# Where the attention masks are added: eight small matmuls per pair of heads' scores, or one VectorE addition on the way to SBUF

## The reference

```python
def local_attention(q, k, v):            # w = WINDOW = 32
    ...
    bk2, bv2 = (look(bk), look(bv))      # keys of the window before, then of this one: 64
    ...
    mask = (it < jb) | (it > jb + w) | (jb == -1)
    sim = jnp.einsum('bhwie,bhwje->bhwij', bq, bk2) * QK_SCALE
    sim = jnp.where(mask, -jnp.finfo(sim.dtype).max, sim)
    attn = jax.nn.softmax(sim, -1)
    out = jnp.einsum('bhwij,bhwje->bhwie', attn, bv2)
```

## Time and profile before

| | before |
|---|---|
| median of three runs | 3484.22 us (3483.04 to 3484.29) |
| profiled execution | 3485.04 us, its span 3483.2 us |
| PE, PE weight loads, DVE, ACT, POOL busy | 3410.3, 2881.8, 2991.3, 3056.1, 2494.3 us |
| granted TensorE clock, mean | 0.997 of full speed |
| scores matmuls L1124, records | 24576, 325.4 us busy |
| mask matmuls L1116 | 3072, 116.8 us busy |
| maxima L1705 | 384, 672 ns each |
| exponentials L1428 | 3072, 343 ns each |

### The profile page before, as it was taken

How to read it: one execution, slowest core, us unless ns; L and a number is a source line. 1 busy time by engine, 2 the same in 40 slices (tenths; PEclk the granted TensorE clock), 3 DMA queues, 4 the chain that set the end, 5 groups by cost and what they waited for, 6 DMA issues and landing times. The chain is left out here.

```text
span 3483.2 us, 177745 instructions
## 1 busy us (share of the span) xinstructions
PE 3410.3 (98%) x70388; PEld 2881.8 (83%) x70388; DVE 2991.3 (86%) x7016; ACT 3056.1 (88%) x10549; POOL 2494.3 (72%) x2057
## 2 busy tenths in 40 slices
PE   8999999999999999999999999999999999999998
PEld 5666677888888888888888888888888888888877
DVE  8999988888888888888888888888888888888886
ACT  8999978898988888888888888888888889888886
POOL 0121178887878878788787887878888788887874
PEclk9999999999999999999999999999999999999999
DMA  2000011111211111121111121111211111111111
GB/s 105 8 5 20 5 53 53 48 42 43 57 55 50 44 44 46 54 57 48 46 44 50 52 57 47 43 42 54 59 48 46 43 47 54 45 46 47 51 42 44
DMA packets 177474, 160.59 MB, mean 46 GB/s; under 512 B 113933, under 2 KB 124813, under 8 KB 176397
## 3 DMA queue, kind: packets, MB, share of 16 engines
q1 hardware_dynamic: 176653, 149.22, 15.2%
HBM read 25.71 MB, written 4.19 MB: 9 GB/s over the span
## 5 line engine op out<-in xcount | busy, mean ns | idle before, releaser
L1544 POOL TENSOR_TENSOR a_rn<-a_ssqc,a_minus_half 128x16 f32<-128x16 f32 x384 | 1113.4, 2900 | 256.3 <-DVE a_ssqc L1751 252.1
L1428 ACT ACTIVATE late<-bank,a_negmax 128x64 f32<-128x64 f32 x3072 | 963.9, 343 | 31.0 <-DVE a_negmax L1705 29.4
L1562 POOL TENSOR_TENSOR a_r<-a_u,a_rn 128x512 f32<-128x512 f32 x768 | 800.7, 1043 | 55.9 <-DVE a_u L1733 10.5
L1428 ACT ACTIVATION_READ_ACCUMULATOR late<-bank,a_negmax 128x1 f32 x3072 | 728.6, 237 | 0.0
L1717 DVE TENSOR_TENSOR a_u<-bank,a_rot_c 128x512 f32<-128x512 f32 x768 | 524.7, 683 | 175.3 <-ACT a_sq L1404 174.7
L1551 POOL TENSOR_TENSOR a_PN<-late,a_erec 128x256 f32<-128x256 f32 x768 | 487.9, 636 | 255.8 <-DVE a_erec L1758 241.4
L1726 DVE TENSOR_TENSOR a_v<-bank,a_rot_s 128x512 f32<-128x512 f32 x768 | 522.7, 681 | 0.0
L1733 DVE TENSOR_TENSOR a_u<-a_u,a_v 128x1024 f32<-128x1024 f32 x384 | 469.7, 1223 | 25.6
L1404 ACT ACTIVATE a_sq<-bank 128x512 f32<-128x512 f32 x768 | 462.8, 647 | 17.2 <-PE bank L1013 16.7
L1411 ACT ACTIVATE a_QK<-bank 128x512 f32<-128x512 f32 x768 | 465.8, 607 | 4.1 <-PE bank L1054 1.9
L1054 PE MATMUL bank<-ident,a_r 128*128 128x128 f32 x3072 | 463.3, 274 | 5.2 <-ACT late L1396 1.8
(11 more groups left out here) (190 smaller groups left out, 7757.2 us busy)
## 6 DMA issues: line engine op xcount, KB each, us to landing
a_V_sh<-a_V_nat SPq DMA_DIRECT2D x384, 192.0 KB, 2.5
a_V_sh<-a_V_nat SPq DMA_DIRECT2D x192, 64.0 KB, 2.4
late<-in_qkv SPq DMA_DIRECT2D x20, 384.0 KB, 3.7
a_x_sh<-X SPq DMA_DIRECT2D x48, 128.0 KB
a_V_sh<-a_V_nat SPq DMA_DIRECT2D x192, 32.0 KB, 2.1
a_x_sh<-X SPq DMA_DIRECT2D x48, 127.0 KB
late<-X SPq DMA_DIRECT2D x47, 128.0 KB
late<-X SPq DMA_DIRECT2D x47, 127.0 KB
```

The source lines that it names most:

```text
L1428: ins = act.activation(E[:, s.par, k, :], scores[:, hp, col:col + KW], ACT.Exp, bias=negmax[:, s.par, k:k + 1], accum_out=esum[:, s.par, k ...
L1544: pool.tensor_tensor(rn[:, a.par, :], ssqc[:, a.par, :], minus_half[:, :], ALU.pow).then_inc(S["rn"], 1)
L1562: pool.tensor_tensor(heads(r[:, a.par, half]), heads(u[:, a.par, half]), rn[:, a.par, mm * 2 * HG:(mm + 1) * 2 * HG].unsqueeze(2).to_broad ...
```

## The change

The eight mask matmuls per pair are gone, and the score matmuls start their own accumulation. DVE adds the mask (now float32, one table for the pairs of a first half and one for the rest) while it moves the scores from `p_s` to `E`; it raises the new semaphore `masked`, waits for it, and takes the maxima from `E`. The exponentials read `E` and write it in place. PE's next scores wait for `masked` in place of `exp1`. The casts of the mask table and of the identity to bf16 ahead of the layers are gone.

```diff
@@ logits (PE) @@
-                    for c in range(4):
-                        for e in range(2):
-                            rows = slice(WIN * c, WIN * c + WIN)
-                            pe.matmul(scores[rows, e, :], ident_b[sides[e], 64 * e:64 * e + WIN],
-                                      masks[sides[e], int(s.half > 0 or c > 0), :], start=True, stop=True, skip_group_check=True)
...
-                                                    QK[sides[e], s.gpar, 2 + hp, first:first + KW], start=False, stop=True,
+                                                    QK[sides[e], s.gpar, 2 + hp, first:first + KW], start=True, stop=True,
@@ cycle (PE) @@
-                    ge(pe, S["exp1"], s.k)
+                    ge(pe, S["masked"], s.k)
@@ exps (ACT) @@
-                        ins = act.activation(E[:, s.par, k, :], scores[:, hp, col:col + KW], ACT.Exp,
+                        ins = act.activation(E[:, s.par, k, :], E[:, s.par, k, :], ACT.Exp,
@@ maxima (DVE) @@
+                    rows = lambda x: x.rearrange("p (b i) k -> p b (i k)", b=2)
                     dve.wait_ge(S["logits"], s.k + 1)
+                    ge(dve, S["pn0"], s.k - 1)
+                    ge(dve, S["pn1"], s.k - 1)
+                    dve.tensor_tensor(rows(E[:, s.par, :, :]), scores, masks[:, int(s.half > 0), :].unsqueeze(1).to_broadcast([P, 2, 4 * KW]),
+                                      ALU.add).then_inc(S["masked"], 1)
+                    dve.wait_ge(S["masked"], s.k + 1)
                     ge(dve, S["exp1"], s.k - 1)
-                    dve.tensor_reduce(negmax[:, s.par, :].rearrange("p (b i) -> p b i", b=2), scores.rearrange("p b (i k) -> p b i k", i=4), AX.X,
-                                      ALU.max, negate=True).then_inc(S["max"], 1)
+                    dve.tensor_reduce(negmax[:, s.par, :], E[:, s.par, :, :], AX.X, ALU.max, negate=True).then_inc(S["max"], 1)
```

More of the change, by code:

```diff
@@ L130, in first_attention @@
         xn = sb("xn", [P, T])
-        masks_f = sb("masks_f", [P, 2, 4 * KW])
         raw = sb("raw", [P, G, 3 * CQ])
@@ L187, in _ @@
                         (w.out[:, :, :], dram["wo"][0]), (A["tabs_c"][:, :, :, :], dram["rot_cos"]),
-                        (A["tabs_s"][:, :, :, :], dram["rot_sin"]), (masks_f[:, :, :], dram["windows"])):
+                        (A["tabs_s"][:, :, :, :], dram["rot_sin"]), (A["masks"][:, :, :], dram["windows"])):
                     sp.dma_start(dst, src).then_inc(S["weights"], 16)
@@ L509, in step @@
                         rotation(dve, A, w, b - 4, half)
-                    if b == 7 and j == F_X + 1:
-                        dve.tensor_copy(A["masks"][:, :, :], masks_f[:, :, :])
-                        dve.tensor_copy(A["ident_b"][:, :], ident[:, :])
                 every_step(dve, step, F_DRAIN)
@@ L647, in layer_constants @@
         sb(n, [P, MT, 2, DH])
-    sb("masks", [P, 2, 4 * KW], BF16)
-    sb("ident_b", [P, P], BF16)
+    sb("masks", [P, 2, 4 * KW])
     sb("x_sh", [P, T])
@@ L737, in all_layers @@
 def all_layers(nc, X, X0, out, ident, psum, banks, A, w, dram, S, kept, late):
-    raw, wh, wl, rot_c, rot_s, masks, ident_b, minus_half = (
-        A[n] for n in ("raw", "wh", "wl", "rot_c", "rot_s", "masks", "ident_b", "minus_half"))
+    raw, wh, wl, rot_c, rot_s, masks, minus_half = (
+        A[n] for n in ("raw", "wh", "wl", "rot_c", "rot_s", "masks", "minus_half"))
     x_sh, xh, xl, sq, ssq, ssqc, rn, u, v, r = (
@@ L1204, in end_logits @@
                 else:
-                    pe.wait_ge(S["exp1"], s.k if j == -4 else s.k - 1)
+                    pe.wait_ge(S["masked"], s.k if j == -4 else s.k - 1)
                 logits(s, end_s(s))
@@ L1420, in values, with exps @@
                                    ACT.Copy).then_inc(S["v_out"], 1)
-            def exps(s, hp, turn, scores):
+            def exps(s, hp, turn):
                 if s:
@@ L1444, in cycle @@
                 queries_and_keys(pair_at(n, p, LAG_Q1), 1)
-                exps(s, 0, 0, p_s)
-                exps(s, 0, 1, p_s)
+                exps(s, 0, 0)
+                exps(s, 0, 1)
                 queries_and_keys(pair_at(n, p, LAG_Q0), 0)
-                exps(s, 1, 0, p_s)
+                exps(s, 1, 0)
                 outputs(pair_at(n, p, LAG_O))
-                exps(s, 1, 1, p_s)
+                exps(s, 1, 1)
                 if p == P_TURN:
@@ L1474, in end_exps @@
                 s = end_pair(j)
-                exps(s, hp, 0, end_s(s))
-                exps(s, hp, 1, end_s(s))
+                exps(s, hp, 0)
+                exps(s, hp, 1)
             def end_gate(f, c, bank):
@@ L1495, in end @@
                 for turn in range(2):
-                    exps(end_pair(-5), 0, turn, p_s)
+                    exps(end_pair(-5), 0, turn)
                 queries_and_keys(end_pair(-2), 0)
-                exps(end_pair(-5), 1, 0, p_s)
+                exps(end_pair(-5), 1, 0)
                 outputs(end_pair(-7))
-                exps(end_pair(-5), 1, 1, p_s)
+                exps(end_pair(-5), 1, 1)
                 end_exps(-4, 0)
@@ L1972, in _ @@
             end()
-LAYER_SEMS = ("xt xh xl x_loaded f_loaded qk_out0 qk_out1 pt pt_out v_out o_out o y pn0 pn1 exp0 exp1 logits r0 r1 "
+LAYER_SEMS = ("xt xh xl x_loaded f_loaded qk_out0 qk_out1 pt pt_out v_out o_out o y pn0 pn1 exp0 exp1 logits masked r0 r1 "
               "qkt0 qkt1 sq0 sq1 qk v max red u u_rot rec0 rec1 rn v_rot0 v_rot1 summed x_out weights w_hi w_lo raw0 raw1 scales "
@@ L2008, in tables @@
     f = np.float32
-    q, k = np.arange(P)[:, None] % 64, np.arange(KW)[None]
+    q, k = np.arange(P)[:, None] % WIN, np.arange(KW)[None]
     seen = (q <= k) & (k <= q + WIN)
-    windows = np.stack([np.concatenate([seen & (k >= WIN), seen] * 2, 1), np.concatenate([seen] * 4, 1)], 1)
+    first, later_on = np.concatenate([seen & (k >= WIN), seen] * 2, 1), np.concatenate([seen] * 4, 1)
+    windows = np.stack([np.where(np.arange(P)[:, None] < WIN, first, later_on), later_on], 1)
     half = np.arange(0, DH, 2, dtype=f)
```

## The result

The kernel after the change takes 3607.53 us (median of four runs, 3604.39 to 3608.93), the kernel before, measured alongside, 3484.26 (3483.04 to 3484.88): a ratio of 1.0353 [1.0337, 1.0369], 123 us slower. 3618 was forecast, in a range of 3560 to 3655.

The account below looks back on a forecast made before the run. PE was taken to bound the kernel before; afterwards the loop through DVE and ACT grows past it. The profiled 3485.0 + 132 for 48 batches + 2 at the end = 3619, less 0.8: 3618 us, range 3560 to 3655.

Parts of the forecast that it names:

- masks' price: PE's time for a pair's eight mask matmuls: 0.12 us, 46 us over 384 pairs if PE stayed the bound.
- (b): Loop from M to the next M through ACT: addition, maxima, exponentials, squares, cosines; 7.03 us, 6.00 before.
- the walk: Position-by-position reckoning through one batch from position 5: 64.3 us instead of 61.57, +2.75.
- (c): M to the next M on DVE's own work alone: 6.47 us, or 7.67 with the statistics of position 1.
- price of 0.03: Extra us assumed for each of eight exponentials reading SBUF instead of PSUM on ACT, 0.24 a pair.
- A2: Rival, chance 0.10: each exponential costs 0.036 us more, 0.29 a pair; 3625 us, or 3634 by the Trainium skill's figure.
- (a): M through DVE's sines and PE's projection to T: no sooner than M + 6.37 us, plus 1.39 in position 4.
- M: Start of DVE's mask addition (before the change, of the maxima); 0.05 us after T if DVE is free.
- T: End of a position's score matmuls on PE, the moment at which the batch is cut into positions.
- B: Rival, chance 0.16: only DVE's own work binds, +1.6 us a batch, 3563 us.
- D: Rival, chance 0.07: PE stays the bound, kernel faster at 3438 us; decided by whether M lags T by over 0.2.
- C: Rival, chance 0.12: weight splits and last batches' statistics on DVE, positions 2 to 5, take the full 0.79; 3640 to 3665.

Follow-up runs that it names:

- seventh kernel: Kernel before, with DVE adding masks only for the pairs of positions 4 and 5, in 31 batches without weight splits, start or end: 3479.83 us, ratio 0.9985.
- second: Changed kernel, but the exponentials read the unmasked scores in PSUM and PE waits for the last exponential again: 3570.16 us, ratio 1.0242.
- third kernel: Changed kernel with addition and maxima in halves of four heads' windows, the first four exponentials waiting only for the first half: 3585.82 us, ratio 1.0287.
- eighth: Changed kernel with one extra 128x512 DVE copy per pair from PSUM to a spare tile, ahead of the masks' addition: 3793.08 us, ratio 1.0885.
- ninth kernel: Changed kernel with one extra 128x512 DVE copy per pair from PSUM, behind the maxima and the sum of squares: 3762.31 us, ratio 1.0794.

## Why the prediction was right

**The bound.** PE sets the pace of the kernel before, and PE's own gain was wanted. Right. The masks' price of 0.12 us a pair holds in a place where PE is the bound: the plain batch of the seventh kernel got 0.09 of it per pair.

**The loop (b).** It is shown: 7.03 us predicted, 7.01 measured, shorter when ACT's part is shorter (second and third kernel), longer by exactly an instruction put into it and not at all by one put beside it (eighth and ninth). It sets the pace in positions 0 and 3 alone, though, and makes 1.13 of the 2.45 us that a plain batch lost. The larger part, 1.34, lies in 1, 2 and 7, where the walk let DVE's own work (c) and the norm decide. Its parts were less good than its sum. Addition to maxima is 0.69 from start to start (2044.03 to 2044.72) for 0.79 predicted, so that DVE's wait for its own result costs less than the 0.11 taken from L1733; maxima to first exponential is 0.72 for 0.69, together 1.41 for 1.48. First exponential to squares is 3.63 for 3.51: each exponential costs 0.045 us more from SBUF, not 0.03. The squares, 0.68 long in the earlier trace rows, released `cosines` 0.61 after their start for 0.70. What these gave and took is -0.07, +0.12, -0.09 and +0.02 (the last behind the cosines). That 7.03 fits so well is luck by half.

**The exponentials.** The price of 0.03 was mis-sized: in the walk's rival A2 it was 0.036, and the measured 0.36 for eight is 0.045 each. The 128x512 copies of the earlier trace rows had shown 36 ns. The Trainium skill, "VectorE: DVE Perf Modes", section "The TRN2 errata — SBUF-src ops pay a fixed extra latency per instruction", has 224 and 172 cycles at 1.2 GHz, an estimate of 43 ns. The trace agrees with it for these instructions. The total of 3634 that went with the dearer exponentials did not come, because the squares and the maxima gave the 0.12 us back.

**The walk (a), (c).** M to T in a position bound by it (1, 2051.04 to 2057.40) was 6.36 us for 6.37 predicted; from the projection to T 2.44 (2054.96 to 2057.40) for 2.35: the first matmul behind a wait takes 0.07 longer to let the next begin, as shown above. Measured from T to T, position 2, where the statistics and the norm stand ahead of PE's transposes, has half of the loss, 1.18 of 2.45 us; 1.36 were predicted. Positions 0 and 4 were forecast 0.17 and 0.21 too long, position 3 0.18 too short. In position 0 it is the start: DVE begins its addition 0.69 behind T (2043.34 to 2044.03), not 0.85. Positions 3 and 4 together are 15.88 for 15.91: what position 2 leaves behind is caught up with in the order in which the walk had it, but one position apart.

**The sum.** Here the forecast was helped by errors that cancel. It had 132 us for 48 batches and 2 for the end; the two traces differ by 124. The 42 intervals from the third `low_x` to the 45th lose 99 us, 2.36 each in the mean: the plain ones 2.45, the two in eight with weight splits 2.67 and 2.87, but one in eight, which took 63.1 us before, only 1.05. The other 25 us lie ahead of them (8), in the last three batches (8; they are 68.78, 68.75 and 68.75 for 66.95, 65.54 and 65.46) and behind (8). At 2.75 a batch the forecast had 116 for the 42, 17 too much, and 18 for the rest, 7 too little; so 3618 lies 10 us above 3607.5.

**The rivals.** B falls with the second, third and eighth kernels, though DVE's own work does decide in positions 1, 2 and 7. D fails on the ground that was given, M behind T: those 0.69 us are far over the 0.2 from which it decides. C's weight splits are real in kind: their batches lose 0.2 and 0.4 us more than a plain one, 3 us in all. That they would cost 20 to 45 us did not come.

**The signs announced.** DVE 90% or more: 90. PE 94 to 96%: 96. PE's L1011 (now L1006) waiting well over 50 us for `v`: 64.7. Light positions about 7.0, position 2 over 8: 7.01 and 8.24. PE's idle time over 40 us: 3607.1 - 3448.0 = 159. This last sign was a poor one: before the change it was 3483.2 - 3410.3 = 73 us already, so that it could hardly have spoken against the forecast.

## What to carry to other kernels

Work taken from the busiest engine pays only where the engine that takes it over, and those in its loop, still keep ahead. Before such an exchange, write down each loop that closes from a stage to its own next turn, waits included, and add the new instructions to those they lie in; a loop that goes through two engines at 86 and 88% can be the next bound though neither is full (here 6.00 us under a position of 6.63, then 7.01). Then make the exchange only in the positions where the loop has room, and leave out those, like start, end and weight-split batches here, where the giving engine already waits. Here that was worth a sixth of a percent.

## What the hardware showed that was not expected

- A float32 exponential of 128x64 with its accumulator starts 0.045 us later behind the one before when it reads SBUF (eight with what follows: 3.63 for 3.27), though its mean length did not grow (339 ns for 343): only the distance of the starts shows it.
- A 128x512 VectorE addition with both inputs in SBUF took up to 0.96 us beside a GpSimd multiplication, and that one up to 1.51 for 1.05; the masks' addition, with one input in PSUM, took 0.667 in the mean with POOL as busy as ever.
- In the ninth kernel a wait of 1.43 us on TensorE, of a position of 7, was followed by a granted clock of 0.62 over 4.5 us, and one of 1.45 us in the batch before by 1.00. Of the 32 middle batches with such a wait 11 had the fall. Waits up to 0.82, in the batch shown of the kernel after the change, left the clock at 1.00.
- TensorE's busy time rose by 38 us with 3072 matmuls fewer. At the one wait worked out, the matmul behind it is longer and the one ahead of it covers a part of it with its tail, 0.22 us of 0.49.
